# Attention from dense edge counts for 896 nodes instead of 768, with 146 gathered steps instead of 154

## The chip, the cores and the metric

The program runs on one core of one Trainium2 chip. The metric is the device time of one execution in microseconds (us). Engine names: TensorE is PE in the views (its weight loads PEld), VectorE is DVE, ScalarE is ACT, GpSimd is POOL, and SP is the queue that issues most transfers.

## The reference, cut to what matters

Four graph layers run over 3125 nodes of 128 features and 103125 edges sorted by destination (50000 pairs in both directions and 3125 self loops). The change lies in the last layer, an attention over the edges with 8 heads of 16 features:

```python
Q, K, V = (x @ Wq + bq), (x @ Wk + bk), (x @ Wv + bv)      # each (n, 8, 16)
score = exp(clip(sum(K[src] * Q[dst], -1) / sqrt(16), -5, 5))   # per edge and head
wV = segment_sum(V[src] * score[..., None], dst)
z = segment_sum(score, dst)
h = layer_norm(x + wV / (z + 0.001), gamma1, beta1)
h = h + relu(layer_norm(h, gamma2, beta2) @ Wo + bo)
```

The result is added to the residual. Edges may repeat, so an edge's weight is multiplied by how often it occurs.

## The kernel before, in words

`build_counts` first builds a table of how many edges run from each source to each destination. `dense_layers` then runs six layers' worth of products with it, in seven passes over 25 node tiles. Pass 6 also makes the keys, values and queries of the attention; for the first DT node tiles it turns the queries as well, and `load_stack` gathers them as a stack in the memory that the counts had. From pass 4 on the counts of the first DN = DT * 128 destinations lie in HBM too (`dense_counts`).

`attention` has two ways to handle an edge.

- **Gathered.** Edges into the later nodes go in steps of 512 edges, six steps (GS) to a group (`step(s, g, j)`: step s, group g = s // 6, place j = s % 6 in it). In a step POOL issues four indirect DMAs (line L1709), each of which fetches the key and value rows of 128 edges. PE spreads the queries to the edges (`aq_bank`), DVE multiplies, makes the one-hot `pick`, reduces and clips the scores and scales the values (L2176, L2180, L2183, L2188, L2193). ACT takes the exponentials (L1784, L1787), copies the next index column (L1728) and makes the query one-hots of the next group with a square and a relu (L1736, L1743). PE sums into `acc_bank` (L1956). After a group come its two norms and its output product, in small pieces of later steps.
- **Dense.** Edges into the first DN nodes aren't gathered. For each of the 25 source tiles (one a group) the scores of all source and destination pairs are taken, head by head, in *units*. In a unit PE computes a score tile into the single bank `score_bank` (L1931, L1934), ACT limits it (`below`, L1755, which frees the bank) and takes its exponential (`power`, L1762), DVE bounds it and multiplies it by the counts (L2202), and PE multiplies it with the values into `value_bank` (L1898, L1901, L1905; in f32, two instructions each). Before, all 12 units of a tile are 512 columns wide: 8 of one head and nodes 0 to 511, and 4 of two heads and nodes 512 to 767. Each step has two.

Within a step the order on ACT is: square, two small exponentials, index copy, `below` of the first unit, one-hot, `power` of the first unit, `below` of the second, the small pieces of older groups, `power` of the second. On PE it is: query spread of step s + 1, score of the first unit, value products of the units of step s - 2, sums of step s - 2, score of the second unit. A unit's score waits until `below` of the unit before it has emptied the bank:

```python
u.count(pe, limited)            # PE: score(g, h) waits for below of the unit before
(u + 1).count(act, scored)      # ACT: below(g, h) waits for its score
```

POOL may run ahead until it needs the buffers: its step s waits for the multiplication of step s - 3. Steps 0 to 143 are written as 12 unrolled steps and a loop of 12 steps 11 times; the rest is written out. The last tile's units stand in steps 144 to 149. Then, by step number: head sums at step 152, then from 154 the output of the dense nodes in two batches (`attended_batch`, `first_norm_batch`, `second_norm_batch`, product, `result_batch`), and the last group from step LAST_AT on.

## Time and profile before

| | us |
|---|---|
| median of 3 runs | 1978.7 (1976.74 to 1980.4) |
| profiled execution, its own time | 1978.04 |
| its span, first to last instruction | 1976.0 |
| dense passes end, attention begins | about 1153 |
| first gather issued | 1154.5 |
| last output store issued | 1970.3 |
| busy share of the whole span | PE 80%, DVE 73%, ACT 62%, POOL 52% |

The span is what the views show; the time is 2.04 us more. All positions below are us from the span's start. The attention is the stretch from 1153 to the end. In a timeline row the first number is the start and the second the busy time. An engine starts its next instruction before the busy time of the last is over, so the distance between two starts is what one costs in a queue without waits.

### The profile page before, as it was taken

How to read it: one execution, taken by the hardware profiler on the slowest of the kernel's cores; microseconds unless marked ns; L12 is line 12 of the kernel's file. 1: busy time of each engine (PE TensorE's matmuls, PEld its weight loads, DVE VectorE, ACT ScalarE, POOL GpSimd, SP SyncE). 2: the span in 40 equal slices, each digit the busy share in tenths (PEclk: the TensorE clock that was granted, in tenths of full speed). 3: DMA queues.
4: the chain of work that ended last, by engine and by line, in shares of the span. 5: the costliest groups of instructions: out<-in, count | busy, mean ns of one | idle time of the engine just before them, and what ended most of it. 6: DMA issues, size and time to landing. Idle time of an engine off the chain costs nothing. (4 is left out here: it accounts for less than half of the span.)

```text
span 1976.0 us, 43645 instructions
## 1 busy us (share of the span) xinstructions
PE 1577.4 (80%) x8528; PEld 992.3 (50%) x8577; DVE 1439.2 (73%) x3748; ACT 1225.3 (62%) x3012; POOL 1029.5 (52%) x1371
## 2 busy tenths in 40 slices
PE   2677776799999898999998938787787787777774
PEld 0233332356555564666665626555565565555552
DVE  7999998644565564333344659889899889899885
ACT  6788887533455332222222359888888888898871
POOL 5644554522454442110134367777777777777770
PEclk9555555999999998999998969999999989999995
DMA  4000000210111124101026464555554555555540
GB/s 163 0 0 0 0 0 16 58 38 28 49 53 48 54 58 136 28 28 36 28 73 131 115 198 145 165 156 151 170 165 142 170 151 157 169 151 157 168 127 18
DMA packets 195400, 182.80 MB, mean 93 GB/s; under 512 B 73341, under 2 KB 167422, under 8 KB 195070
## 3 DMA queue, kind: packets, MB, share of 16 engines
q1 hardware_dynamic: 165758, 101.21, 17.7%
q0 software_dynamic: 29568, 80.78, 14.1%
q8 instruction: 25, 0.41, 0.1%
q14 instruction: 49, 0.40, 0.1%
HBM read 145.35 MB, written 32.87 MB: 90 GB/s over the span
## 5 line engine op out<-in xcount | busy, mean ns | idle before, releaser
L1709 POOL DMA_INDIRECT counts<-keys_values,a_index x596 | 564.2, 947 | 181.6 <-issue 162.1
L997 PE MATMUL z_bank<-y_parts,counts 128*128 128x384 bf16 (+1 forms) x3658 | 643.0, 328 | 1.2 <-DVE y_parts L1357 0.6
L997 PEld LDWEIGHTS z_bank<-y_parts,counts 128*128 (+1 forms) x3658 | 358.7, 98 | 229.0 <-issue 5.8
L444 POOL TENSOR_TENSOR key_low_build<-iota_b_build,src_cols_build 128x768 bf16<-128x768 bf16 x102 | 155.1, 1521 | 148.4 <-DVE flat_build L524 128.9
L1762 ACT ACTIVATE counts<-counts,a_five 128x512 f32<-128x512 f32 x300 | 214.3, 714 | 7.3
L1755 ACT ACTIVATE counts<-score_bank,a_five 128x512 f32<-128x512 f32 x300 | 201.4, 671 | 24.3 <-PE score_bank L1934 17.0
L1248 DVE TENSOR_REDUCE z_sum<-z_bank 128x128 f32<-128x384 f32 x150 | 83.6, 557 | 177.4 <-PE z_bank L997 173.2
L2202 DVE SCALAR_TENSOR_TENSOR counts<-counts,counts_bank 128x512 f32<-128x512 f32 x300 | 193.3, 679 | 7.7 <-ACT counts L1762 7.1
L1956 PEld LDWEIGHTS acc_bank<-counts 128*128 128x128 f32 x1232 | 172.2, 197 | 48.7 <-issue 32.9
L1871 PE MATMUL aq_bank<-counts 126*128 126x128 bf16 x616 | 61.5, 223 | 161.0 <-DVE counts L2176 147.6
L1898 PE MATMUL value_bank<-counts 128*128 128x512 f32 x350 | 183.7, 645 | 1.3
L1956 PE MATMUL acc_bank<-counts 128*128 128x136 f32 x1232 | 173.8, 285 | 3.9 <-DVE counts L2188 3.9
L620 PE MATMUL share_build<-flat_build,src_tile_build 128*128 128x275 bf16 x408 | 108.2, 422 | 73.7 <-ACT src_tile_build L586 40.9
L542 DVE TENSOR_TENSOR counts<-share_build,counts 128x275 f32 x408 | 155.2, 439 | 7.8 <-PE share_build L620 5.7
L2176 DVE TENSOR_TENSOR counts<-aq_bank,counts 128x512 f32<-128x512 f32 x154 | 106.0, 688 | 60.0 <-DMA counts<-keys_values,a_index 49.6
L524 DVE TENSOR_TENSOR flat_build<-iota_wide_build,src_cols_build 128x2200 bf16<-128x2200 bf16 x102 | 147.8, 1450 | 1.2
L1106 ACT ACTIVATE hT<-t_bank 128x128 f32<-128x128 f32 x175 | 48.3, 276 | 157.1 <-PE t_bank L964 152.0
L620 PE MATMUL share_build<-flat_build,left_build 128*128 128x275 bf16 x408 | 108.4, 423 | 42.8 <-ACT left_build L586 39.8
L1871 PEld LDWEIGHTS aq_bank<-counts 126*128 126x128 bf16 x616 | 39.3, 98 | 197.8 <-issue 169.6
L1114 ACT ACTIVATE y_parts<-d_bank 128x128 f32 (+1 forms) x150 | 41.1, 274 | 145.5 <-PE d_bank L978 145.4
L978 PE MATMUL d_bank<-weights,hT 128*128 128x256 f32 x350 | 114.7, 410 | 19.1 <-ACT hT L1106 18.4
L579 ACT ACTIVATE key_low_build<-key_low_build 128x768 bf16<-128x768 bf16 x102 | 85.9, 842 | 56.0 <-POOL key_low_build L444 56.0
(248 smaller groups left out, 2842.5 us busy)
## 6 DMA issues: line engine op xcount, KB each, us to landing
counts<-group_rel_rows SPq DMA_DIRECT2D x26, 768.0 KB, 4.7
self_term<-s_out SPq DMA_DIRECT2D x150, 64.0 KB, 1.6
s_in<-self_term SPq DMA_DIRECT2D x150, 64.0 KB, 1.8
counts<-keys_values,a_index POOLq DMA_INDIRECT x596
residual<-x_in SPq DMA_DIRECT2D x75, 64.0 KB, 1.6
dense_counts<-counts SPq DMA_DIRECT2D x1, 4800.0 KB, 14.4
counts<-key_parts_turned SPq DMA_DIRECT2D x50, 96.0 KB
counts<-dense_counts SPq DMA_DIRECT2D x25, 192.0 KB
```

The lines of the kernel that those rows point to most:

```text
L444: nc.gpsimd.tensor_tensor(square[:, g.slot(), :, :].rearrange("p (h c) n -> p h c n", h=2)[:, :, 0:BY_POOL, :], place.unsqueeze(1).unsquee ...
L524: nc.vector.tensor_tensor(right[:, g.slot(), :, :, :], iota_wide[:, :, :].unsqueeze(1).to_broadcast([P, 2, KW, 4]), keys.unsqueeze(2).to_b ...
L542: nc.vector.tensor_tensor(window, share[GB * j + i][:, 0:KW].rearrange("p (t w) -> p t w", w=WP), window, ALU.add).then_inc(column_sums, 1)
L620: ins = nc.tensor.matmul(share[j * GB + i][:, 0:KW], left[j][:, i % 2 * GB + c, :], right[:, j, i % 2, :, c], start=c % 2 == 0, stop=c % 2 ...
L978: ins = nc.tensor.matmul(out_[:, 0:2 * D], hT[:, n.slot(), :], weights[p % 2][:, :], start=True, stop=True)
L997: return nc.tensor.matmul(bank(p, dt)[:, 0:width], counts[:, bass.ds(dt.value(P) + source * NA, P)], y3[(p - 1) % 2][:, source, 0:width], ...
L1709: nc.gpsimd.indirect_dma_start(rows_kv[:, j, c, :], None, v.kv, bass.IndirectOffsetOnAxis(column, 0)).then_inc(gathered[j], 16)
L1755: nc.scalar.activation(room_below[:, u.slot(), :], score_bank[:, :], ACT.Relu, bias=five[:, :], scale=-1.0).then_inc(limited, 1)
L1762: nc.scalar.activation(weighted[u.slot(PR)], room_below[:, u.slot(), :], ACT.Exp, bias=five[:, :], scale=-1.0).then_inc(powered, 1)
L1898: ins = nc.tensor.matmul(value_bank[0][:, :], placed(h), weighted[u.slot(PR)], start=False, stop=last and h == ALONE - 1)
L1956: ins = nc.tensor.matmul(acc_bank[:, 0:TW], pick[:, s2.slot(MR), c, :], msg[:, s2.slot(MR), c, :], start=j == 2 and c == 0, stop=False)
L2202: nc.vector.scalar_tensor_tensor(now, now, LOWEST, edges, ALU.max, ALU.mult).then_inc(weighed, 1)
```

## The change

DT goes from 6 to 7 (destinations 0 to 895 are dense), SKIP from 48 to 56 (8 steps fewer are gathered, and 25 groups are left of 26). Nodes 512 to 895 are 384 columns, so a tile now has 8 units of 512 columns and 8 of 384, one head each, 16 in all. `OF_STEP` deals them over the six steps as 3, 3, 2, 2, 3, 3; a third unit's `below` and `power` stand at the end of ACT's step. Six score-weight buffers become eight. The batches at the end have 4 and 3 tiles, and the two first norms use two fused operations where there were three. The stack of queries and the dense counts get 896 columns.

```diff
-DT = 6
+DT = 7
-SKIP = 48
+SKIP = 56
...
-    UNITS = 2 * GS
+    UNITS = 2 * H
+    OF_STEP = ((0, 1, 2), (3, 4, 5), (6, 7), (8, 9), (10, 11, 12), (13, 14, 15))
-    BATCH = DT // 2
+    BATCHES = ((0, 4), (4, DT))
-    PR = 6
+    PR = 8
...
+        def nodes(h):
+            return WIDE if h < H else SIDE
...
-            return [(g, 2 * j), (g, 2 * j + 1)] if tile(g) else []
+            return [(g, u) for u in OF_STEP[j]] if tile(g) else []
...
-            for i in range(PAIR * (TURNS + 1), LAST_AT + 6):
+            for i in range(PAIR * (TURNS + 1), max(LAST_AT + 6, TILES_AT + 5)):
...
-                nc.scalar.activation(room_below[:, u.slot(), :], score_bank[:, :], ACT.Relu, bias=five[:, :], scale=-1.0).then_inc(limited, 1)
+                nc.scalar.activation(room_below[:, u.slot(), 0:nodes(h)], score_bank[:, 0:nodes(h)], ACT.Relu, bias=five[:, :],
+                                     scale=-1.0).then_inc(limited, 1)
...
                 for _, h in now[1:2]:
                     power(s, g, h)
+                for _, h in now[2:3]:
+                    below(s, g, h)
+                    power(s, g, h)
...
-                elif h == ALONE:
-                    for n in range(2):
-                        ins = nc.tensor.matmul(value_bank[1][:, SIDE:2 * SIDE], placed(h, n), half(n), start=False, stop=False)
+                elif h % H == ALONE:
+                    for n in range(nodes(h) // P):
+                        ins = nc.tensor.matmul(value_bank[1][:, SIDE:WIDE], placed(ALONE, h // H * WIDE_TILES + n),
+                                               weighted[u.slot(PR)][:, n * P:n * P + P], start=False, stop=last and n == DT - WIDE_TILES - 1 and h > H)
                 else:
-                    for n, i in enumerate(pair_of_heads(h)):
-                        at = SIDE if i == ALONE else 0
-                        ins = nc.tensor.matmul(value_bank[1][:, at:at + SIDE], placed(i, 2 if i == ALONE else None), half(n),
-                                               start=False, stop=last and i == ALONE)
+                    ins = nc.tensor.matmul(value_bank[1][:, 0:SIDE], placed(h - H), weighted[u.slot(PR)][:, 0:SIDE], start=False, stop=False)
...
-                for _, h in now[1:2]:
+                for _, h in now[1:3]:
                     score(g, h)
...
-                chain.step(normed(h2_now, h1[:, :], 0))
-                chain.step(nc.vector.tensor_tensor(h2_now, h2_now, gamma1[:, :], ALU.mult))
-                chain.step(nc.vector.tensor_tensor(h2_now, h2_now, beta1[:, :], ALU.add))
+                chain.step(nc.vector.scalar_tensor_tensor(h2_now, h1[:, :], stat[:, 0, MV.start:MV.start + 1], gamma1[:, :], ALU.subtract, ALU.mult))
+                chain.step(nc.vector.scalar_tensor_tensor(h2_now, h2_now, stat[:, 0, RSTD:RSTD + 1], beta1[:, :], ALU.mult, ALU.add))
```

How the instructions stand, at two places. On ACT, the last step of a group in the unrolled part (j = 5), before: `a_apart` is the square, `score_bank` the source of `below`, `a_five` with `counts` on both sides `power`.

```order
L1736 ACTIVATE a_apart<-counts,a_query_lane 128x512
L1784 ACTIVATE place_bank<-a_clipped 128x32
L1787 ACTIVATE counts<-a_clipped 128x4x8
L1728 ACTIVATE a_index<-a_src 128x4
L1755 ACTIVATE counts<-score_bank,a_five 128x512
L1743 ACTIVATE counts<-a_apart,a_one 128x512
L1762 ACTIVATE counts<-counts,a_five 128x512
L1755 ACTIVATE counts<-score_bank,a_five 128x512
L1762 ACTIVATE counts<-counts,a_five 128x512
```

The same step of the change:

```order
L1740 ACTIVATE a_apart<-counts,a_query_lane 128x512
L1789 ACTIVATE place_bank<-a_clipped 128x32
L1792 ACTIVATE counts<-a_clipped 128x4x8
L1732 ACTIVATE a_index<-a_src 128x4
L1759 ACTIVATE counts<-score_bank,a_five 128x384
L1747 ACTIVATE counts<-a_apart,a_one 128x512
L1767 ACTIVATE counts<-counts,a_five 128x384
L1759 ACTIVATE counts<-score_bank,a_five 128x384
L1767 ACTIVATE counts<-counts,a_five 128x384
L1759 ACTIVATE counts<-score_bank,a_five 128x384
L1767 ACTIVATE counts<-counts,a_five 128x384
```

A third pair has joined the step, each `power` directly behind its own `below`. On PE, the third and fourth steps (j = 2 and 3), before: `aq_bank` is the query spread, `value_bank` the value products of the units two steps back, `acc_bank` the sums.

```order
L1871 MATMUL aq_bank<-counts 128x128 x4
L1931 MATMUL score_bank<-counts 128x512
L1898 MATMUL value_bank<-counts 128x512 x2
L1956 MATMUL acc_bank<-counts 128x136 x4
L1931 MATMUL score_bank<-counts 128x512
L1871 MATMUL aq_bank<-counts 128x128 x4
L1934 MATMUL score_bank<-counts 128x256 x2
```

The same place of the change:

```order
L1878 MATMUL aq_bank<-counts 128x128 x4
L1932 MATMUL score_bank<-counts 128x512
L1901 MATMUL value_bank<-counts 128x512 x3
L1956 MATMUL acc_bank<-counts 128x136 x4
L1932 MATMUL score_bank<-counts 128x512
L1878 MATMUL aq_bank<-counts 128x128 x4
L1934 MATMUL score_bank<-counts 128x384
```

Between the two scores of a step now stand three value products of 512 columns instead of two.

## Rows read from the trace of the kernel before

**Rows 1.** Busy time by stretch: window, length, engines, PE clock, DMA share, GB/s.

```profile
1200.00:1400.00 200.00, 155.79 (x861) 110.70 (x873) 179.84 (x421) 173.66 (x405) 151.28 (x160) 0.96 0.56 161
...
1600.00:1800.00 200.00, 154.66 (x860) 111.08 (x872) 181.05 (x427) 171.67 (x401) 151.25 (x161) 0.96 0.54 157
```

**Rows 2.** Groups by form, 1200 to 1800: busy us, mean ns | idle before.

```profile
L1709 POOL DMA_INDIRECT counts<-keys_values,a_index x480 | 454.3, 946 | 146.3 <-issue 131.3 <-DVE counts L2176 7.6 <-ACT a_index L1728 6.1
```

**Rows 3.** Who waited, 1200 to 1800: us in total, times, longest.

```profile
ACT place_bank L1784 <- DVE a_clipped L2193: 49.1, 60, 2.4
DVE counts L2176 <- DMA counts<-keys_values,a_index: 36.4, 40, 1.6
ACT counts L1755 <- PE score_bank L1934: 14.5, 10, 2.4
```

**Rows 4.** Timeline of ACT in a step without waits.

```profile
1896.29 0.71 ACT L1736 ACTIVATE a_apart<-counts,a_query_lane 128x512 bf16<-128x512 bf16 x1
...
1897.24 0.67 ACT L1755 ACTIVATE counts<-score_bank,a_five 128x512 f32<-128x512 f32 x1
1897.81 0.71 ACT L1743 ACTIVATE counts<-a_apart,a_one 128x512 bf16<-128x512 bf16 x1
1898.42 0.71 ACT L1762 ACTIVATE counts<-counts,a_five 128x512 f32<-128x512 f32 x1
1899.04 0.67 ACT L1755 ACTIVATE counts<-score_bank,a_five 128x512 f32<-128x512 f32 x1
1899.80 0.72 ACT L1762 ACTIVATE counts<-counts,a_five 128x512 f32<-128x512 f32 x1
1900.43 0.71 ACT L1736 ACTIVATE a_apart<-counts,a_query_lane 128x512 bf16<-128x512 bf16 x1
```

**Rows 5.** Groups by form, whole span: one ACT form at two widths, DVE at 512 and 384.

```profile
L1821 ACT ACTIVATE counts<-at_bank,a_beta,a_gamma 128x128 f32<-128x128 f32 x26 | 11.6, 448 | 5.2 <-PE at_bank L1978 5.2
L1851 ACT ACTIVATE counts<-score_bank,a_beta,a_gamma 128x384 f32<-128x384 f32 x2 | 1.3, 670 | 7.0 <-PE score_bank L2006 7.0
L2202 DVE SCALAR_TENSOR_TENSOR counts<-counts,counts_bank 128x512 f32<-128x512 f32 x300 | 193.3, 679 | 7.7 <-ACT counts L1762 7.1
L2161 DVE SCALAR_TENSOR_TENSOR counts<-value_bank,counts 128x384 f32<-128x384 f32 x2 | 1.1, 558 | 5.7 <-PE value_bank L2000 5.7
```

**Rows 6.** Timeline: PE at full clock, then the wait after a slow stretch.

```profile
1425.35 1.88 PE L1898 MATMUL value_bank<-counts 128*128 128x512 f32 x4
1427.07 1.09 PE L1956 MATMUL acc_bank<-counts 128*128 128x136 f32 x8
1427.99 0.38 PE L1934 MATMUL score_bank<-counts 128*128 128x256 bf16 x2
...
1431.86 1.91 PE L1898 MATMUL value_bank<-counts 128*128 128x512 f32 x2
...
1436.00 0.69 ACT L1755 ACTIVATE counts<-score_bank,a_five 128x512 f32<-128x512 f32 x1 [1.15 <-PE score_bank L1934]
```

**Rows 7.** Timeline: first gather, head-sum transposes, first and last batch operation, last store.

```profile
1154.47 1.23 POOL L1709 DMA_INDIRECT counts<-keys_values,first_index  x1 [3.46 <-issue]
...
1926.52 1.09 PE L1964 MATMUL value_bank<-ident,counts 128*128 128x128 f32 x8 [0.92 <-ACT counts L1806]
...
1936.91 0.14 DVE L2124 TENSOR_SCALAR counts<-counts 128x24 f32<-128x24 f32 x1
...
1965.39 0.56 DVE L2162 TENSOR_TENSOR counts<-counts 128x384 f32<-128x384 f32 x1
...
1970.26 0.34 SPq L1637 DMA_DIRECT2D out<-counts  x1
```

**Rows 8.** The chain that ended last, at the attention's start.

```profile
1169.51 0.72 ACT a_apart L1736
```

**Rows 9.** Timeline of DVE in pass 6, where the query stack is loaded.

```profile
1072.12 0.56 DVE L1248 TENSOR_REDUCE z_sum<-z_bank 128x128 f32<-128x384 f32 x1 [1.45 <-PE z_bank L997]
1081.04 0.35 DVE L1254 SCALAR_TENSOR_TENSOR layer_out<-z_sum,inv_count,s_in 128x128 f32<-128x128 f32 x1 [8.36 <-DMA s_in<-self_term]
```

More of the change, by code:

```diff
@@ L1962, in step @@
                     pe.wait_ge(sums_ready, 2)
-                    for i in range(DT + 2):
+                    for i in range(DT + 1):
                         ins = nc.tensor.transpose(tile_bank(i), head_sums[i // 4][:, i % 4 * P:i % 4 * P + P], v.ident[:, :])
@@ L2095, in moments_of_batch @@
             def moments_of_batch(x, b):
-                for i in range(BATCH):
-                    chain.start(nc.vector.bn_stats(tile_stat[:, b * BATCH + i, BN], x[:, i, :]))
+                now = tile_stat[:, of_batch(b), :]
+                for i in range(size(b)):
+                    chain.start(nc.vector.bn_stats(now[:, i, BN], x[:, i, :]))
                 chain.settle()
-                for i in range(BATCH):
-                    ins = nc.vector.bn_aggr(tile_stat[:, b * BATCH + i, MV], tile_stat[:, b * BATCH + i, BN])
-                    if i < BATCH - 1:
+                for i in range(size(b)):
+                    ins = nc.vector.bn_aggr(now[:, i, MV], now[:, i, BN])
+                    if i < size(b) - 1:
                         chain.start(ins)
@@ L2127, in attended_batch @@
                     dve.wait_ge(tiles_ld, 64)
-                for i in range(BATCH):
+                for i in range(size(b)):
                     chain.start(nc.vector.tensor_tensor(h1_now[:, i, :].rearrange("p (h d) -> p h d", h=H),
@@ L2139, in first_norm_batch @@
                 refine_batch(b)
-                for i in range(BATCH):
-                    chain.start(normed_of_batch(h2_all[b], h1_all[b], b, i))
+                now = tile_stat[:, of_batch(b), :]
+                for i in range(size(b)):
+                    chain.start(nc.vector.scalar_tensor_tensor(h2_all[b][:, i, :], h1_all[b][:, i, :], now[:, i, MV.start:MV.start + 1],
+                                                               gamma1[:, :], ALU.subtract, ALU.mult))
                 chain.settle()
-                chain.step(nc.vector.tensor_tensor(h2_all[b], h2_all[b], gamma1[:, :].unsqueeze(1).to_broadcast([P, BATCH, D]), ALU.mult))
-                chain.step(nc.vector.tensor_tensor(h2_all[b], h2_all[b], beta1[:, :].unsqueeze(1).to_broadcast([P, BATCH, D]), ALU.add))
+                for i in range(size(b)):
+                    chain.start(nc.vector.scalar_tensor_tensor(h2_all[b][:, i, :], h2_all[b][:, i, :], now[:, i, RSTD:RSTD + 1],
+                                                               beta1[:, :], ALU.mult, ALU.add))
+                chain.settle()
                 moments_of_batch(h2_all[b], b)
@@ L2150, in second_norm_batch @@
                 refine_batch(b)
-                for i in range(BATCH):
+                for i in range(size(b)):
                     ins = normed_of_batch(h1_all[b], h2_all[b], b, i)
-                    if i < BATCH - 1:
+                    if i < size(b) - 1:
                         chain.start(ins)
@@ L2231, in step @@
                     result_batch(b)
-            over_steps(step, chain, 2 * 15)
+            over_steps(step, chain, 2 * 14)
             tail(step)
```

77 lines of the change are left out of this document (36 added, 41 removed).

## The prediction

> **What bounds the kernel now.** I read the busy time by stretch first, because the change lies in the attention and a share over the whole span says little about it. From 1200 to 1800 every stretch of 200 us looks the same: DVE works 180 us, ACT 172 to 174, POOL 151 and PE 155 [rows 1]. So it is a steady state, no engine is full, and busy time alone names no bound. The group of the gathers does. In 600 us POOL issues 480 indirect DMAs, one every 1.25 us, 0.946 us of work and 0.30 us of idle time before each, nearly all of which is "issue", which is waiting for nothing [rows 2]. POOL never stops: four gathers are 5.00 us a step and 30.0 us a group. All 616 gathers at that rate take 770 us from the first at 1154.5 [rows 7], which ends at about 1925. The attention is paced by POOL's issue of gathers.
>
> The waits agree. DVE waits for landed gathers, 36.4 us in 20 groups, and ACT waits for DVE's clipped scores, 49.1 us [rows 3]. They are the slack of these two engines, 1.8 and 2.5 us a group. The third row is the one to remember: ACT waits for PE's score tile, 14.5 us in 10 waits, up to 2.4 us each. The timeline shows where they come from. At full clock PE does two value products (four instructions) in 1.72 us, start to start, so 0.86 us each, the sums in 0.92 and a score in 0.38. At 1431.86 two instructions take 1.91 where they took half before, the clock is down to its lower level (1.2 of 2.4 GHz), and a little later ACT waits 1.15 us for the next score [rows 6]. Before the change the slack swallows that.
>
> **The change, part by part.** *POOL.* 8 steps of 4 gathers go: 32 x 1.25 = 40.0 us less. If POOL still set the pace, this would be the gain. The question is whether ACT, DVE and PE can do a tile of 16 units in POOL's 30.0 us.
>
> *ACT.* A step without waits runs from 1896.29 to 1900.43, 4.14 us, start to start [rows 4]. Six are 24.8, and the small pieces of a group (one copy, one turned tile, two square roots by logarithm and exponential) add about 1.3, my estimate: 26.1 us a group. The stretches give 25.9 us busy [rows 1], and 30.0 less the two waits of [rows 3] leaves at most 26.8. In the same step `below` costs 0.57 and `power` 0.61, start to start, at 512 columns [rows 4]. No unit is 384 columns wide. The nearest rows are one form at 128 and 384 columns, 448 and 670 ns, so 0.11 us for each 128 columns [rows 5]; a unit of 384 then costs 0.46 + 0.50 = 0.96. The ends are nothing saved (1.18) and a saving in proportion to the width (0.89). 12 units at 1.18 were 14.2 us; 8 at 1.18 and 8 at 0.96 are 17.1: +3.0. The third pair of a step stands alone, and `power` directly behind its own `below` starts 0.76 us after it, where another instruction would start after 0.61 [rows 4]: four times 0.15, +0.6. ACT's own work is then 29.7 us a group, 0.3 under POOL's pace.
>
> The Trainium skill (VectorE: DVE Perf Modes, on the fixed extra latency of SBUF sources in trn2) gives a fixed cost per instruction and one cycle per column for ScalarE, and advises tiles of 512 or more. [Rows 5] agree in kind: three times the columns cost 1.5 times the time. By its cycle counts the 384-column pair is 0.97 us, which as an estimate makes the sum 0.1 us a group longer; its advice speaks against four more and narrower units a tile.
>
> *ACT and PE in turn.* There is one score bank, so PE and ACT alternate on it. After a step of three units, PE can only put the first score of the next step when the third `below` is done. Then come the value products, the sums and the second score. Where three products of 512 columns lie between (j = 2 and 3) that is 0.38 + 3 x 0.86 + 0.92 + 0.38, less the overlap of the first score with the products (about 0.15): 4.1 us [rows 6]. In that time ACT has `power` 0.63, square and three small ones 0.95, `below` 0.57, one-hot 0.61 and `power` 0.62, and 0.1 for the hand-over: 3.5 us [rows 4]. ACT waits 0.6 to 0.7 us at both places: +1.3 a group. With two products it was 3.2 us, under ACT's time. At j = 0 the transposition for an older group now stands behind the third score on PE, and ACT's copy of it behind the second `below`: a score and a transposition, about +0.6.
>
> The sum is 26.1 + 3.0 + 0.6 + 1.3 + 0.6 = 31.6 us a group. That is over POOL's 30.0: POOL stops pacing, it waits for DVE's products, and the gain of 40 us is no longer on the path. The ends are 30.0 (POOL's pace holds) and 32.7 (ACT's base 26.8, and half of the 0.7 us a group that the slow-clock waits of [rows 3] cost once no slack is left, with a little for DVE).
>
> *DVE.* It is busy 27.1 us a group [rows 1]. Four more products by the counts at no more than 0.68 and 0.12 less for each of eight narrow ones [rows 5] add 1.8; the fused norm takes 0.3 off: 28.6. It has less slack but doesn't bound. Transfers grow by 32 KB a tile against a DMA share of 0.54 to 0.56 [rows 1]: nothing.
>
> *The end of the attention.* ACT's first step begins at 1169.5 [rows 8]. 24 groups at 31.6 are 758.4: 1927.9. The last tile's six steps have no squares and one-hots (12 x 0.61 less) and few gathered parts, but the same turns on the score bank without the cover of other work; 28 us, bounds 24 and 31: 1955.9. Its last value products come 3 us later: 1958.9. Before, the head sums, their transposition and the short copies lay beside the last gathers; now no gathers are left, the sums wait for the last unit, and all of it is exposed: two copies 1.1, seven transposes at 1.09 / 8 [rows 7], 16 short copies about 1.9: 4 us, 1962.9. From the first batch operation to the end it was 1936.91 to 1976.0, 39.1 us. The last group's output then followed the batches, its store 4.9 us behind the last batch operation [rows 7]; now it is done ahead of them. Seven tiles for six in these chains cost about 3 us: 37 us, and the end is at 1999.9.
>
> *Pass 6.* The load of the query stack held DVE for 8.36 us, between 1072.12 and 1081.04 [rows 9]. A sixth more bytes make that 1.4 longer, and a seventh tile with turned queries 0.4: +1.8, ends 0 and 4. The larger store of dense counts in pass 4 waits for nobody: 0.
>
> The span is then 2001.7. The profiled execution took 2.04 us more than its span and is 0.7 under the median of the runs, so I leave that out: **2004 us**, 25 over the median of 1978.7, 1.3% slower.
>
> **The rivals.**
>
> *POOL keeps the pace, faster.* For it: ACT's own work adds up to 29.7, under 30.0, and waits seen once in a hand-made sum can be filled by other waits. Against it: the turns on the score bank come on top, and every one of ACT's 0.3 us of slack would have to hold. Price: 24 x (31.6 - 30.0) = 38 us less, 1966. The point from which it decides is 30.55 us a group, where the time is that of before.
>
> *Slower still.* The clock of PE goes on dropping (0.96 and 0.97 in the mean, [rows 1]), and each drop is now paid in full, or the narrow units save little of ACT's time (0.22 less for each is what the sum has). 32.6 us a group: 24 us more, 2028. For it: the 10 waits of [rows 3] in 600 us. Against it: PE has more to do and shorter idle spells.
>
> *DVE becomes the bound.* It would have to need 3 us more than the 28.6; its products by the counts wait for ACT but don't lengthen. It gives no time of its own and I leave it in the second rival.
>
> **How the numbers follow.** A measurement of this kernel can tell 0.2% (4 us) from no change. The forecast with 30.9 to 32.1 us a group (1987 to 2016) has a chance of 0.58, the faster rival up to 30.7 us (1964 to 1983) 0.22, the slower one 0.20. Of the faster rival's 0.22, 0.06 lie within 4 us of before. So faster 0.16, same 0.06, slower 0.78. The range leaves one in ten on either side: 1970, well into the faster rival, to 2031, just beyond the slower one.
>
> **What would show it.** Right: gathers at 1.25 us apart only in part, POOL waiting for DVE's products and the last gather ending near 1918 instead of 1885; starts of the shift operation (once a group) 31.6 us apart; ACT busy over 90% of the stretch and its wait for clipped scores nearly gone; PE waiting for `below` and ACT for scores at j = 2 and 3; the head sums some 35 us after the last gather. Wrong: groups 30.0 us apart and ACT still waiting for clipped scores (POOL's pace), or a narrow `below` or `power` at more than 0.6 us. A clock below 0.95 in the steady stretch would be the slower rival.

## The result, and the profile after

The changed kernel takes **2035.9 us** (median of 3 runs, 2035.2 to 2038.3) against 1978.7: the ratio is 1.029, with a 95% interval of 1.027 to 1.030. It is 57 us slower. The prediction had 2004 and a range to 2031. Its profiled execution has a span of 2034.3 us.

Start with the cadence. The shift operation of DVE runs once a group, so the first and the last start in its row (by source line) give the length of a group. The timeline of POOL has the first gather.

```profile
L2042 DVE TENSOR_TENSOR counts<-a_iota,a_shift_col x25: 279/282/285, 1172.1 to 1958.6; 128x128 f32<-128x128 f32 x25
```

```profile
1160.43 1.23 POOL L1713 DMA_INDIRECT counts<-keys_values,first_index  x1 [3.47 <-issue]
```

(1958.6 - 1172.1) / 24 = **32.8 us a group**, where the prediction had 31.6. The first of these intervals is the longest, 35.6; counted by ACT's own instructions a group takes 32.6. The gathers begin 6.0 us later than before [rows 7].

The busy time by stretch of the changed kernel (columns as in [rows 1]), and the waits from 1200 to 1800 us in total, times and longest:

```profile
1200.00:1400.00 200.00, 156.66 (x836) 102.36 (x848) 171.87 (x400) 180.57 (x419) 140.11 (x149) 0.98 0.51 146
...
1600.00:1800.00 200.00, 156.53 (x845) 102.10 (x856) 174.81 (x406) 181.03 (x420) 140.89 (x149) 0.99 0.50 147
```

```profile
DVE counts L2206 <- ACT counts L1767: 56.4, 75, 2.2
PE score_bank L1934 <- ACT counts L1759: 54.8, 92, 1.0
PE score_bank L1932 <- ACT counts L1759: 53.2, 57, 1.3
POOL counts L1713 <- DVE counts L2181: 52.0, 48, 2.8
...
ACT counts L1759 <- PE score_bank L1932: 19.8, 24, 1.7
ACT counts L1759 <- PE score_bank L1934: 13.5, 18, 0.8
ACT counts L1825 <- PE at_bank L1978: 10.7, 18, 0.6
```

POOL fell from 151 to 140 of 200 us and now waits for DVE: it no longer paces. ACT rose from 173 to 180, DVE fell from 180 to 173 and now waits for ACT's exponentials (L1767; 1.1 us before), and ACT's wait for clipped scores, 49.1 us in [rows 3], is gone. PE waits for ACT's limiting (L1759) and ACT for PE's scores: both sides of one bank wait for each other, and neither engine is full.

Where in a group does ACT wait? The timeline of ACT repeats almost exactly from group to group. A wait of 0.59 for the turned tile stands in step j = 0, one of 0.54 for a score at j = 2, one of 0.75 at j = 3. In 8 of the 24 intervals there is also one of 1.7 us at j = 1.

```profile
1502.70 0.69 ACT L1759 ACTIVATE counts<-score_bank,a_five 128x512 f32<-128x512 f32 x1
1503.98 0.46 ACT L1825 ACTIVATE counts<-at_bank,a_beta,a_gamma 128x128 f32<-128x128 f32 x1 [0.59 <-PE at_bank L1978]
...
1514.30 0.71 ACT L1767 ACTIVATE counts<-counts,a_five 128x512 f32<-128x512 f32 x1
1515.55 0.69 ACT L1759 ACTIVATE counts<-score_bank,a_five 128x512 f32<-128x512 f32 x1 [0.54 <-PE score_bank L1932]
...
1518.98 0.60 ACT L1767 ACTIVATE counts<-counts,a_five 128x384 f32<-128x384 f32 x1
1520.33 0.58 ACT L1759 ACTIVATE counts<-score_bank,a_five 128x384 f32<-128x384 f32 x1 [0.75 <-PE score_bank L1934]
...
1542.90 0.69 ACT L1759 ACTIVATE counts<-score_bank,a_five 128x512 f32<-128x512 f32 x1 [1.71 <-PE score_bank L1932]
```

The idle time in brackets is counted from the end of the busy time, but ACT starts an instruction before that end. What a wait costs is therefore the distance from start to start, less the same distance where nothing waits. For the turned tile that is 1.28 - 0.57 = 0.71 us, for the score at j = 2 it is 1.25 - 0.61 = 0.64, and at j = 3 it is 1.35 - 0.51 = 0.84 (0.57 and 0.61 as in [rows 4]; 0.51 is a narrow exponential without a wait in the same timeline). Two more delays carry no bracket: 0.18 us at j = 0 and 0.12 at j = 1, each at a second limiting. Added up like this, ACT loses 2.5 us in this group and 2.7 in the one before it.

PE's timeline shows the same four value instructions at the same step of two neighbouring groups, and the granted clock of these moments (third column from the end) shows the rest:

```profile
1505.68 0.39 PE L1932 MATMUL score_bank<-counts 128*128 128x512 bf16 x1 [1.28 <-ACT counts L1759]
1505.91 1.45 PE L1907 MATMUL value_bank<-counts 128*128 128x384 f32 x4
...
1537.69 0.44 PE L1932 MATMUL score_bank<-counts 128*128 128x512 bf16 x1 [1.30 <-ACT counts L1759]
1537.92 2.77 PE L1907 MATMUL value_bank<-counts 128*128 128x384 f32 x4
```

```profile
1504.00:1508.00 4.00, 2.72 (x18) 1.86 (x16) 3.20 (x7) 3.91 (x10) 2.86 (x4) 1.00 0.35 99
1537.90:1542.50 4.60, 4.60 (x20) 3.33 (x18) 3.77 (x7) 3.29 (x8) 3.38 (x5) 0.63 0.36 110
```

1.45 us at full clock, 2.77 at mostly the lower level (0.63 in the mean), directly after PE had waited 1.30 us for ACT. In the group without the drop PE had waited as long, 1.28 us, so this wait alone does not bring it. A group without such a drop takes 31.7 or 32.4 us in turn, 32.1 in the mean; one with it takes 33.3 to 34.1.

The dense part: in pass 6 two tiles are 19.0 us apart where the query stack is loaded (1080.09 to 1099.13), where DVE waited 8.36 us before [rows 9] and waits 10.87 now.

```profile
1080.09 0.56 DVE L1248 TENSOR_REDUCE z_sum<-z_bank 128x128 f32<-128x384 f32 x1 [1.11 <-PE z_bank L997]
1091.52 0.35 DVE L1254 SCALAR_TENSOR_TENSOR layer_out<-z_sum,inv_count,s_in 128x128 f32<-128x128 f32 x1 [10.87 <-DMA s_in<-self_term]
1099.13 0.56 DVE L1248 TENSOR_REDUCE z_sum<-z_bank 128x128 f32<-128x384 f32 x1 [4.47 <-PE z_bank L997]
```

### The profile page after: what moved, and what is told of

Same layout as the page of the kernel before. It is cut to its first block and busy times, and to the rows that moved or that the text cites. A ratio compares the mean times of both kernels' runs of the same rounds, so it can differ in the third digit from the quotient of the medians.

```text
span 2034.3 us, 44278 instructions
## 1 busy us (share of the span) xinstructions
PE 1629.9 (80%) x8632; PEld 984.8 (48%) x8681; DVE 1450.2 (71%) x3772; ACT 1304.2 (64%) x3179; POOL 1000.3 (49%) x1342
## 5 line engine op out<-in xcount | busy, mean ns | idle before, releaser
L1713 POOL DMA_INDIRECT counts<-keys_values,a_index x564 | 533.6, 946 | 231.4 <-issue 162.8
L2206 DVE SCALAR_TENSOR_TENSOR counts<-counts,counts_bank 128x512 f32<-128x512 f32 (+1 forms) x400 | 235.6, 615 | 97.6 <-ACT counts L1767 87.1
L1759 ACT ACTIVATE counts<-score_bank,a_five 128x512 f32<-128x512 f32 (+1 forms) x400 | 247.9, 620 | 56.9 <-PE score_bank L1932 31.6
L1767 ACT ACTIVATE counts<-counts,a_five 128x512 f32<-128x512 f32 (+1 forms) x400 | 264.6, 661 | 17.0
L1956 PEld LDWEIGHTS acc_bank<-counts 128*128 128x128 f32 x1168 | 153.7, 191 | 36.6 <-issue 23.9
L1901 PE MATMUL value_bank<-counts 128*128 128x512 f32 x350 | 162.4, 592 | 1.3
L1956 PE MATMUL acc_bank<-counts 128*128 128x136 f32 x1168 | 159.4, 279 | 0.0
L1907 PE MATMUL value_bank<-counts 128*128 128x384 f32 x350 | 134.7, 516 | 15.9 <-ACT counts L1759 15.0
L1934 PE MATMUL score_bank<-counts 128*128 128x384 bf16 x200 | 66.5, 333 | 75.1 <-ACT counts L1759 74.9
L1932 PE MATMUL score_bank<-counts 128*128 128x512 bf16 x151 | 59.9, 397 | 77.2 <-ACT counts L1759 77.1
```

The costliest lines, as they stand in the source:

```text
L1713: nc.gpsimd.indirect_dma_start(rows_kv[:, j, c, :], None, v.kv, bass.IndirectOffsetOnAxis(column, 0)).then_inc(gathered[j], 16)
L1759: nc.scalar.activation(room_below[:, u.slot(), 0:nodes(h)], score_bank[:, 0:nodes(h)], ACT.Relu, bias=five[:, :], scale=-1.0).then_inc(lim ...
L1767: nc.scalar.activation(weighted[u.slot(PR)][:, 0:nodes(h)], room_below[:, u.slot(), 0:nodes(h)], ACT.Exp, bias=five[:, :], scale=-1.0).the ...
L1901: ins = nc.tensor.matmul(value_bank[0][:, :], placed(h), weighted[u.slot(PR)], start=False, stop=last and h == ALONE - 1)
L1907: ins = nc.tensor.matmul(value_bank[1][:, 0:SIDE], placed(h - H), weighted[u.slot(PR)][:, 0:SIDE], start=False, stop=False)
L1956: ins = nc.tensor.matmul(acc_bank[:, 0:TW], pick[:, s2.slot(MR), c, :], msg[:, s2.slot(MR), c, :], start=j == 2 and c == 0, stop=False)
```

## Experiments

**The theory** is that PE and ACT take turns on the one score bank, and that their waits for each other come on top of ACT's own work (a). The rivals are that ACT's own instructions set the pace and the waits are only what they leave over (b), and that DVE or POOL does (c).

**Two score banks.** A second bank needs a free PSUM bank. The first way is to put the node numbers, the upper limit and the weights, which had one, in SBUF; `places_sbuf` does that alone.

```diff
-        (place_bank,) = ps("place_bank", 1)
-        places, upper = place_bank[:, 0:P], place_bank[:, P:P + 1]
+        places, upper = sb("a_places", [P, P]), sb("a_upper", [P, 1])
+        weights = sb("a_weights", [P, 2 * GC * H]).rearrange(...)
```

> The changed kernel with the node numbers, the upper limit and the exponentiated scores of the gathered edges (weights) in SBUF instead of a PSUM bank of their own. It is the control for the kernel with two score banks, which needs that bank. DVE reads one of these three in three instructions a step. Turns on the score bank (my theory: PE and ACT alternate on it, and the waits come on top of ACT's own work) and ACT's own work alone both expect 2036 within 4 us and the shift operation 32.8 us apart, because DVE is not on the path. If DVE's time is on the path, three reads a step that become slower by some 0.05 us each lengthen a group by 0.9 us: 2057.

Measured: 2041.6 (2 runs, ratio 1.031), groups 32.9. The 6 us are small against what follows.

```diff
-        (score_bank,) = ps("score_bank", 1)
+        score_banks = ps("score_bank", 2)
-                u.count(pe, limited)
+                (u - 1).count(pe, limited)
-                matmul(score_bank[:, :], ...)
+                matmul(score_banks[u.slot()][:, :], ...)
```

> As the control with all in SBUF, and the freed PSUM bank is a second score bank: unit u uses bank u mod 2, and a score waits for the limiting of unit u-2 instead of u-1. Turns on the score bank: PE no longer stands between two limitings, ACT's waits for scores (33.3 us in 1200 to 1800, 1.8 us a group) fall to under 8 us, a group takes 31.0 us (bounds 30.6 and 31.4), the time is 2036 - 24 x 1.8 = 1993 (bounds 1983 and 2003). ACT's own work sets the pace and the waits are only what it leaves over: the group stays over 32.4, time over 2026. POOL cannot go below 30.0 a group in either.

Measured: **1982.3** (ratio 1.0013, interval 1.0002 to 1.0024), 59 us under its control, groups (1912.6 - 1171.9) / 24 = 30.9. Its waits for scores from 1200 to 1800:

```profile
ACT counts L1759 <- PE score_bank L1932: 2.5, 2, 1.3
```

33.3 us (35.4 in the control) have become 2.5, and the granted clock is 0.99 to 1.00. The expectation had 1993, with 1983 as its lower bound; a group lost 2.1 us instead of 1.8, because most of the clock drops went too (behind the first group, 3 groups still have a wait of over 1 us for a score, where the changed kernel has 8), and the end after the last shift operation shrank from 77.1 to 69.5 us. ACT, DVE and POOL do the same work in both kernels, so this is (a), against (b) and (c). POOL's idle time before a gather is back at 0.305 us in the mean, as in [rows 2]: at two banks POOL sets the pace again.

**PE's part of the turn.** `values_128` narrows 14 of 16 value products (the narrow units' in the same way as the wide units' shown here).

```diff
-  matmul(value_bank[0][:, :], placed(h), weighted[u.slot(PR)], ...)
+  matmul(value_bank[0][:, 0:P], placed(h), weighted[u.slot(PR)][:, 0:P], ...)
```

> The changed kernel with the value products of 14 of the 16 units narrowed to 128 of their 512 or 384 columns; the other columns' values are left out. It takes about 0.6 us of PE's time from each of these units and nothing from ACT, DVE or POOL. Turns on the score bank: between the first and the second score of a step PE then needs 2 us and less than ACT, ACT's waits for scores go down to those of the third unit, a group takes 31.0 (bounds 30.6 and 31.6), the time is 1993 (1983 to 2007), the tail a little shorter. ACT's own work alone: 32.8 a group and 2034 stay. If TensorE's granted clock falls because it has less to do, part of the gain is lost, and the profile would show the clock.

Measured: 2023.6 (2 runs, 2019.4 and 2027.8), groups 32.6. A miss, and the profile says why it decides little:

```profile
1400.00:1600.00 200.00, 135.11 (x857) 106.53 (x855) 174.22 (x406) 179.87 (x419) 140.26 (x149) 0.88 0.50 146
```

PE is busy 22 us less of 200, and its granted clock fell from 0.97 to 0.88. ACT's waits for scores halved (17.9 us), but others took their place in part (8.0 for clipped scores, which were none; 12.3 for the turned tile, which were 10.7).

**ACT's part.** `act_384`: both ACT instructions of every unit at 384 columns.

> The changed kernel with both ACT instructions of every unit at 384 columns, also of the eight units that have 512 nodes (the last 128 nodes are left out there). It takes 8 x 0.22 = 1.8 us a group of ACT's work and nothing from PE or DVE. ACT's own work alone: a group falls by the whole 1.8 to 31.0 and the time by 42 us to 1994. Turns on the score bank: where PE is the longer side of the turn (the steps with three value products, at j = 2 and 3) the shorter instruction only makes ACT wait longer, two to four of the eight wide units lie there, so a group falls by 0.9 to 1.4 to 31.4 to 31.9, time 2002 to 2014, and ACT's waits for scores grow to 45 us or more in 1200 to 1800.

Measured: 2013.2 (2 runs, ratio 1.017), groups (1937.4 - 1173.4) / 24 = 31.8, 0.94 less for 1.8 us less work. ACT's waits grew from 33.3 to 54.0:

```profile
ACT counts L1759 <- PE score_bank L1932: 37.7, 57, 2.0
...
ACT counts L1759 <- PE score_bank L1934: 16.3, 19, 0.9
```

(a) as expected, and more clearly than the mean says. Groups without a clock drop take 31.1 or 31.8 us in turn, 31.5 in the mean, 0.6 less than the 32.1 of the changed kernel; so two thirds of what ACT saved became waiting for PE. The other 0.3 of the 0.94 are drops: 3 of 24 groups had one here, 8 there.

**The order on PE.** `score_ahead` has the second score ahead of the value products, one bank.

> The changed kernel with one score bank; PE computes the second score of a step ahead of the value products and the sums instead of behind them. It then waits for ACT's first limiting in front of the products. If it is the three value products between two scores that make ACT wait: ACT's waits for scores (33.3 us in 1200 to 1800) fall to 10 us or less, a group takes 31.4 to 32.0 (32.8 now), 2010 to 2020. If what counts is the whole of PE's program behind a wait on the bank: the waits move to PE, the products and sums come later, a group stays at 32.6 to 33.5, 2030 to 2055.

Measured: 2231 (one run), groups 40.8: far outside both. ACT's waits for scores rose to 100.3 us, and PE's for the limiting to 169.6. With one bank PE stands in front of the second score until ACT has limited the first, with products, sums and the next spread behind it. So it is PE's whole program behind a wait on the bank that counts, and the expectation's price for that was much too low. PE's granted clock was lower too, 0.87 to 0.88; what part of the 8 us a group is the clock's, this run doesn't separate.

**The clock.** `spread_twice` fills PE's idle time with a repeated product.

> The changed kernel with every product that spreads a step's query rows over its edges computed twice (four more small matmuls a step, 0.4 us of PE's time; the result is the same). PE has 1.3 us of idle time behind them, waiting for ACT's third limiting, in the step where in 8 of 22 groups its clock drops and ACT then waits 1.7 us for a score. If PE's idle time brings the drops: the granted clock is 1.00 in 1200 to 1800, no wait of 1.7 us is left, groups take 32.1 us instead of 32.8 and the time is 2020 (bounds 2016 to 2026). If the drops have nothing to do with it: same pattern of waits, 2036 (2032 to 2042). If PE's total work is on the path more than I think, each step gains 0.4 us: up to 2090.

Measured: 2042.2 (2 runs, ratio 1.032). Groups without a drop take 32.3; there is no drop from 1400 to 1600 (clock 1.00), but those at both ends stayed, 6 in all instead of 8. Neither of the first two cases; the 0.2 us a group more is PE's work (ACT's wait at j = 2 is 0.77 us and not 0.54). What brings the drops stays open.

**The fused normalisation alone.** `before_fused` puts it into the kernel before.

> The kernel before with only the small part of the change: the first normalisation of a group in two DVE instructions instead of three (not in the batches at the end). DVE works 0.3 us a group less. POOL's issue paces the kernel before: the same time within 4 us (1975 to 1983). If DVE is on the path, up to 0.3 x 25 = 7 us less, 1972.

Measured: 1977.3 (10 runs) against 1979.0, ratio 0.999 (0.998 to 1.000). This part of the change costs nothing.

**The query stack.** `stack_768` loads `[:, 0:6 * P]` of the seven tiles' columns.

> The changed kernel with only 768 of the 896 columns of the query stack loaded at the end of the dense part (the last 128 nodes' queries are left out): eight loads of 192 KB as before, but the seventh tile is still turned. In the changed kernel two tiles are 19.0 us apart there, 16.0 before. If the 256 KB more do it: 16.0 to 17.0 apart, DVE's wait for s_in 8 to 9 us instead of 10.9, the last groups and all else as in the changed kernel, 2033 us. If it is where the loads stand or the seventh tile's work: 18.5 to 19.5 apart, 2036 us.

Measured: the two tiles are 16.2 us apart, and the first gather is at 1157.14, 3.3 us earlier than in the changed kernel:

```profile
1079.66 0.56 DVE L1248 TENSOR_REDUCE z_sum<-z_bank 128x128 f32<-128x384 f32 x1 [1.10 <-PE z_bank L997]
1088.72 0.35 DVE L1254 SCALAR_TENSOR_TENSOR layer_out<-z_sum,inv_count,s_in 128x128 f32<-128x128 f32 x1 [8.51 <-DMA s_in<-self_term]
1095.85 0.56 DVE L1248 TENSOR_REDUCE z_sum<-z_bank 128x128 f32<-128x384 f32 x1 [3.97 <-PE z_bank L997]
```

The 256 KB more cost 2.8 us there. The end is no earlier, 2038.2 in the one run: the first group took 37.7 us instead of 35.6, 9 groups had a clock drop instead of 8, and the part behind the last shift operation took 77.6 us instead of 75.7.

**A surprise, and its control.** The kernel before with two banks, numbers in SBUF:

> The kernel before (12 units a source tile) with the same two score banks and nothing else. POOL's issue paces it, and ACT had slack for the 14.5 us of waits for scores: the same time within 4 us, 1976 to 1983. If the turns on the score bank had held the kernel before too, it would gain at least half of what the changed kernel gains from the second bank (59 us): 1950 or less.

Measured: 2005.5 (2 runs, ratio 1.013), slower, which no theory had. Some of its gathers took up to 1.45 us; hence `before_places_sbuf`:

> The kernel before (one score bank, 12 units) with the node numbers, the upper limit and the weights in SBUF: the control for the kernel before with two score banks, which took 2005 instead of 1980. In that one, some gathers took 1.2 to 1.44 us on POOL instead of 0.95, those that start while DVE compares edges and node numbers (both operands in SBUF now). If DVE's SBUF operands hold POOL back: 2000 to 2010 here too, with gathers of up to 1.45 us and a mean over 0.98. If the second score bank itself slows the kernel before: 1979 within 5 us here.

Measured: **2002.6** (2 runs, ratio 1.012) with one bank. What moved to SBUF does it. The timeline of a held gather:

```profile
1223.49 0.95 POOL L1708 DMA_INDIRECT counts<-keys_values,a_index  x1 [0.30 <-issue]
...
1224.67 0.68 DVE L2179 TENSOR_TENSOR counts<-a_rel,a_places 128x512 f32<-128x512 f32 x1
1224.74 1.42 POOL L1708 DMA_INDIRECT counts<-keys_values,a_index  x1 [0.30 <-issue]
1225.27 0.68 DVE L2182 TENSOR_REDUCE a_score<-counts 128x32 f32<-128x512 f32 x1
```

Of the 465 gathers that begin from 1200 to 1800, 71 begin while DVE compares edges with node numbers (L2179), and 53 of these take over 1.1 us; of the 394 others none does. The 53 are exactly those that begin in the first 0.4 us of the comparison, and each ends 1.5 us after the comparison's start: the earlier it begins, the longer it is held. In the kernel before, with the numbers in PSUM, none of 480 gathers takes over 1.1 us, though 29 of them begin in the first 0.4 us of the comparison. What the gathers of these 600 us take above 0.946 us each adds up to 20.1 us; over the 770 us of gathers that would be 26, near the 24 measured.

**More changes at two banks, numbers in SBUF.** `two_banks_order` has ACT limit the third unit before the second exponential; `two_banks_384` narrows ACT.

```diff
-                for _, h in now[1:2]:
-                    power(s, g, h)
                 for _, h in now[2:3]:
                     below(s, g, h)
+                for _, h in now[1:3]:
                     power(s, g, h)
```

> The kernel with two score banks, and in ACT's program the third limiting of a step stands ahead of the second exponential (below, below, power, power instead of below, power, below, power; four buffers for what is limited instead of two). No exponential of a third unit then stands directly behind its own limiting, which cost 0.15 us each by my sum, 0.6 us a group. ACT still close to the path: a group takes 30.1 to 30.4 instead of 30.86, the time is 1970 (bounds 1964 and 1976). POOL has taken over the pace again (its gathers stand 1.25 us apart nearly everywhere in the kernel with two banks): only what the groups have over 30.5 can go, 1978 to 1984. POOL's floor is 24 x 30.0.

> The changed kernel with two score banks and both ACT instructions of every unit at 384 columns (the last 128 nodes of the wide units are left out): the same edit that took 0.94 us off a group with one bank. With two banks POOL paces (gathers 1.25 us apart, some longer): a group stays at 30.3 to 30.9, and the time falls only by the last tile's share, 1976 to 1984. If ACT's work still sets the pace with two banks, a group falls by another 0.8 or more, but not under 30.0: 1955 to 1965.

Measured: 1993.2 (4 runs, 1.006) and 1994.9 (2 runs, 1990.4 and 1999.4; 1.008), both *slower* than 1982.3 though each takes work or a stall from ACT. The mean gather is 1000 and 994 ns, against 970 in `two_banks`, and the idle time before a gather is 0.305 us in all three. So POOL is the bound, and when its gathers meet the comparison decides: from 1200 to 1800, 55 and 48 gathers are held for over 1.1 us, against 14 in `two_banks`.

**Two banks with the numbers in PSUM.** The turned tile and the projection move into spare columns of the bank of the sums, between one group's last sum and the next one's first, so that their bank is free. Two things move with them: DVE's result of a group stands earlier in its step, and PE computes a step's third score behind the turned tile instead of ahead of it.

```diff
-        t_bank, c_bank = small_bank[:, 0:P], small_bank[:, P:P + D]
+        t_bank, c_bank = acc_bank[:, 2 * P:3 * P], acc_bank[:, 3 * P:3 * P + D]
-                if j == 0 and early(g2):
+                if j == 1 and early(g2):
                     turn_over(g2)
-                if j == 1 and early(g2):
+                if j == 2 and early(g2):
                     project(g2)
+                        (g2 + 1).count(pe, res_ready)   # before the group's first sum
```

> The changed kernel with a second score bank, and the node numbers, the limit and the weights in PSUM as in the changed kernel. The second bank is that of the turned tile and the projection, which now lie in spare columns of the bank of the sums; they are computed one step later, between the end of one group's sums and the start of the next one's, and DVE's result of a group stands in the middle of its step. No comparison of DVE reads two operands of SBUF, so no gather may take over 1.1 us. If POOL's pace is all that is left: gathers 1.25 us apart, groups 30.0 to 30.4, and 24 x 0.6 = 14 us less than with the numbers in SBUF (1982): 1968 (bounds 1964 and 1975), faster than the kernel before. If ACT's own work (its busy time is 29.4 a group, with four exponentials directly behind their own limiting 30.0) holds the groups too: 30.6 to 31.0, 1978 to 1988. If the projection and the result, now tighter, make PE wait at the third step: 31 or more, over 1988.

> The same, and in ACT's program the third limiting of a step ahead of the second exponential, with four buffers for what is limited. With the numbers in SBUF this order was 11 us slower than the other (1993 against 1982), which I put down to more gathers held by DVE's comparison. If so, here it is not slower: 1962 to 1970, groups 30.0 to 30.3. If the order itself is bad (DVE gets a step's second unit later): again 8 us or more over two_banks_psum.

> The kernel before (12 units) with the same second score bank, all else in PSUM as before. POOL paces it and no gather is held: 1979 within 4 us. If the turns on the bank (14.5 us of waits for scores in 600 us) cost the kernel before something: up to 10 us less.

Measured: 2032.5, 2013.2 and 1978.3. The last is the control: with 12 units this change is worth nothing (10 runs, ratio 0.9997, interval 0.9987 to 1.0007). ACT's waits for scores even grew in it, from 16.9 to 39.5 us, and cost nothing while POOL paces. The two kernels with the numbers in SBUF say the same (2005.5 with two banks, 2002.6 with one). With 16 units the size of the expectation's third case came true, but with DVE and not PE waiting, for the projection (two_banks_psum):

```profile
DVE counts L2099 <- PE acc_bank L1958: 61.4, 17, 3.6
```

The order on ACT now gained 19 us, with no gather held: it was not the order that was bad above. Then DVE's result was put one step later (`two_psum_later`), with the other order on ACT too (`two_psum_later_order`):

```diff
-                if j == 2 and early(g - 2):      # behind the clipping
+                if j == 3 and early(g - 2):      # behind the comparison
                     result(g - 2)
```

> two_banks_psum with DVE's result of a group 3.2 us later in its program: at the fourth step, behind the comparison of edges and nodes, instead of in the middle of the third. DVE then waits for the projection under 0.5 us instead of 3.6. Turns on the score bank were what the 16 units lost, and POOL paces what is left: groups 30.0 to 30.6, 1968 (1962 to 1980), faster than the kernel before. ACT's own work holds the groups: 30.8 to 31.4 (its busy time of 29.4, 0.7 for exponentials behind their own limiting, 0.6 for other waits), 1984 to 2000. The wait only moves to PE or to ACT: over 31.5, over 2002.

> The same, with the third limiting ahead of the second exponential in ACT's program (four buffers for what is limited). In the pair two_psum_order and two_banks_psum this was worth 19 us, 0.75 a group, at a pace over POOL's. If two_psum_later is at 30.0 to 30.3, POOL's pace, nothing is left to gain here, within 4 us of it; if it is above, this is lower by up to 0.7 a group and not under 30.0: 1962 to 1975.

Measured: 2008.6 (groups 31.8) and 1988.4 (1.004, groups 31.0). DVE's wait is gone; ACT now waits 1.2 us a group for the second score of j = 2, behind the sums (20.6 and 22.1 us in 600). `two_psum_last` takes that score ahead of the sums:

```diff
+                for _, h in now[1:2] if j == 2 else []:
+                    score(g, h)
                 if sub(s2):      # the sums
...
-                for _, h in now[1:2]:
+                for _, h in now[1:2] if j != 2 else []:
                     score(g, h)
```

> two_psum_later_order with one thing more: in the third step of a group PE computes the second score ahead of the sums, which wait there for DVE's result. ACT's wait of 1.2 us for this score goes. If ACT then has only its own work left (30.87 - 1.15 = 29.7 a group), POOL sets the pace, groups take 30.0 to 30.3 and the time is 1988 - 24 x 0.7 = 1971 (1966 to 1976), faster than the kernel before. If PE is then late with the spread of the next step and ACT waits elsewhere: 30.6 or more, 1982 to 1990.

Measured: **1966.3** (5 runs), ratio 0.993, interval 0.992 to 0.995: faster than both kernels. Groups take (1895.0 - 1172.2) / 24 = 30.1 us, and POOL paces again, waiting for hardly anything else (10.7 us for DVE, 4.9 for ACT; stretch, then waits):

```profile
1400.00:1600.00 200.00, 163.69 (x913) 109.67 (x925) 186.28 (x441) 186.47 (x450) 151.28 (x161) 1.00 0.55 158
```

```profile
POOL counts L1714 <- issue: 129.1, 424, 0.3
```

161 gathers in 200 us are 1.24 us each, and POOL's busy time is that of [rows 1]. ACT's waits for scores are not nil (25.5 us in 21), but now they fit in ACT's slack.

## Why the prediction was wrong in size

**What bounds the kernel, and where it goes: right.** POOL stopped pacing, ACT stood at 90%, the wait for clipped scores went, PE and ACT waited for each other. The experiments show that the single score bank is the cause: the second one takes 59 us from the changed kernel (`two_banks` against `places_sbuf`) and nothing from the kernel before.

**Where the 32.6 us lie.** The forecast span was 2001.7, the measured one 2034.3. The sum counts from ACT's first step, so I count there too:

```profile
1174.06 0.72 ACT L1740 ACTIVATE a_apart<-counts,a_query_lane 128x512 bf16<-128x512 bf16 x1 [0.67 <-DMA counts<-group_rel_rows]
...
1175.02 0.67 ACT L1759 ACTIVATE counts<-score_bank,a_five 128x512 f32<-128x512 f32 x1
...
1957.59 0.67 ACT L1759 ACTIVATE counts<-score_bank,a_five 128x512 f32<-128x512 f32 x1
```

The first row is the start of ACT's first step, the two others are the first limiting of the first and of the last source tile. The step begins 2.8 us later than forecast (1169.5 + 1.8). The 24 groups take 1957.59 - 1175.02 = 782.6 us, 32.6 each, and not 758.4: 24.2 more. What follows takes 77.7 us and not 72: 5.7 more. In the group's sum two terms failed, the turns and the clock. The shift operation's first interval of 35.6 us is no term of its own: ACT's first two groups take 33.0 and 31.1.

**ACT and PE in turn: right in kind, too small by 0.7. This is the first step that failed.** The sum had 0.6 to 0.7 us at j = 2 and at j = 3 and 0.6 at j = 0, 1.9 together. The bracketed waits, 0.54, 0.75 and 0.59, also add up to 1.9, but that agreement is an accident of how they are counted. From start to start, as the sum was made, the three places cost 0.64, 0.84 and 0.71, and with the two delays that the sum didn't have it is 2.5 to 2.7 a group. That is 17 us in 24 groups.

**ACT's own work: slightly too large.** A group without a clock drop took 32.1 us; less 2.6 for the turns leaves 29.4 to 29.5, where the sum had 29.7. The widths by form:

```profile
L1767 ACT ACTIVATE counts<-counts,a_five 128x512 f32<-128x512 f32 x147 | 105.2, 716 | 6.8
L1759 ACT ACTIVATE counts<-score_bank,a_five 128x512 f32<-128x512 f32 x147 | 99.3, 676 | 22.4 <-PE score_bank L1932 19.8 <-remote 0.5
L1767 ACT ACTIVATE counts<-counts,a_five 128x384 f32<-128x384 f32 x149 | 90.4, 607 | 5.4
L1759 ACT ACTIVATE counts<-score_bank,a_five 128x384 f32<-128x384 f32 x149 | 83.9, 563 | 13.5 <-PE score_bank L1934 13.5
```

128 columns less save 0.109 and 0.113 us; the 0.11 taken from [rows 5] holds. The price of a fixed cost per instruction that the Trainium skill gives (VectorE: DVE Perf Modes, the note on SBUF sources in trn2) is borne out by these rows too: a quarter fewer columns take the exponential from 716 to 607 ns, 15% less. Two errors of the sum cancel in part. An exponential behind its own limiting starts 0.76 us after it where another instruction starts after 0.57, so it costs 0.19 and not 0.15 (the sum took 0.61, the price of the exponential, from 0.76). And the small pieces of a group, put at 1.3 by estimate, cost 0.8 from start to start.

**The clock: the second step that failed.** The text had it as the reason of the slower rival and as the upper bound of 32.7, with half of 0.7 us a group; in the sum it stood at nothing. It cost 8 drops of 1.67 us, 13 us in all or 0.56 a group. The argument against it ("PE has more to do and shorter idle spells") was half right: the mean granted clock rose, from 0.96 and 0.97 to 0.97 to 0.99, so the sign that the text gave for the slower rival, a clock below 0.95, did not show. But the drops that were left were now paid in full. Why some groups have one is not known: PE waits 1.3 us for ACT at j = 1 in groups with a drop and in groups without. A price like this belonged in the sum once ACT had no slack left, not in a rival.

**Pass 6: +1.8 forecast, 3.0 measured** (19.0 us between two tiles, where it was 16.0 from 1072.12 on; 2.8 of it are the bytes, by `stack_768`). The larger store of dense counts "waits for nobody: 0" was not right either: the kernels are 1.7 us apart ahead of it and 2.6 behind the next pass's first tiles, so it costs 0.9. The 1.7 arose before, most of it near 530 us, where this profile has PE's clock at 0.89 and that of before at 1.00; the change has no part there. Together the dense part is 6.0 us longer, 4.2 more than forecast. ACT's first step gets 1.4 of them back, because it waits 0.67 us for the rows of its group and not 2.66 as before. This is not exact: in other runs with this dense part the first shift operation came at 1169.4 to 1175.7 us, 1172.1 here.

**DVE: 28.6 forecast, not bound: right, but too high.** It was busy 173 of 200, 28.3 a group of 32.8. **The tail: too short by 5.7.** The last tile took 31.1 us and not 28 (the text's upper bound was 31). From there to the first batch operation (1995.8) it was 8.1 and not 7, and the batches to the end took 38.5 and not 37. 2.8, 24.2 and 5.7 are the 32.6 us.

**The rivals.** "POOL keeps the pace, faster" was wrong for this kernel, by the waits on the bank, but right in its number: 1966 is what the tiling gives when the second bank and the order of the programs take them away (`two_psum_last`, 1966.3; this kernel still has a longer dense part, so the agreement to the microsecond is chance). "Slower still" is nearest to what happened, and right in its group of 32.6 us. Of its two reasons only the first came true, and only for half of the 1.0 us; the other half is the turns, which it didn't name. Its 2028 was passed by the start and the tail.

## What to carry to other kernels

Before trading work of one engine (40 us of gathers here) for work of another, list the single buffers between the engines that get the new work: a buffer of one makes their times add up where they had overlapped, and its waits, harmless while another engine paces, are paid in full from then on. Price a second buffer in the same breath, with what has to move to make room for it: of the versions tried here only the last beat the kernel before, the others gave part of the gain back, or nearly all of it, through held gathers or a new wait. And measure a group's pace over many groups with rare events in it (a clock drop in every third), not on one clean step.

## What the runs showed of the hardware that was not expected

A gather of POOL that begins in the first 0.4 us of DVE's comparison of two operands in SBUF (128 x 512, 0.68 us) is held until 1.5 us after the comparison's start. It takes 1.13 to 1.44 us instead of 0.95, in 53 of 53 cases of `before_places_sbuf`; with one of the operands in PSUM it never did, in 29 cases. In the kernel before, having them in SBUF costs 24 us (2002.6 against 1979.0). Whether every DVE instruction with two SBUF operands does this is open: in `two_banks` none of the 74 gathers that began in the product of SBUF rows with the SBUF weights was held, but they began in its first 0.03 us or after 0.4 us, and none in between, where the comparison holds them.

And PE's granted clock was lower with the value products narrowed, 0.88, than without, 0.97 to 0.99.
